# Last-layer messages of a graph network: the maximum with zero written in the form that also writes an accumulator

## What is computed

```python
src, dst = (edge_index[0], edge_index[1])
msg = jax.nn.relu(x[src] + edge_attr)
agg = jax.ops.segment_sum(msg, dst, num_segments=x.shape[0])
h = x + (x + agg)
f = _bn(h, bn1_gamma, bn1_beta, bn1_mean, bn1_var)
f = jax.nn.gelu(f @ W1.T + b1, approximate=False)
f = f @ W2.T + b2
return _bn(h + f, bn2_gamma, bn2_beta, bn2_mean, bn2_var)
```

## Time and profile before

| | |
|---|---|
| median of 3 runs | 7266.05 us (7260.23 to 7266.66) |
| profiled execution, its own time | 7249.92 us |
| its span, first to last instruction | 7247.8 us |
| busy share of the span: GpSimd (POOL) | 71% |
| TensorE (PE) | 63% |
| VectorE (DVE) | 37% |
| ScalarE (ACT) | 11% |

### The profile page before, as it was taken

The page is one execution under the profiler, slowest core; times in us unless marked ns, Lnnn a source line. Parts: engine busy times, 40 slices in busy tenths (PEclk is TensorE's granted clock), DMA queues, the critical chain, the costliest instruction groups (busy, mean ns, idle before and its releaser), DMA issues.

```text
span 7247.8 us, 61408 instructions
## 1 busy us (share of the span) xinstructions
PE 4554.3 (63%) x16502; PEld 3357.7 (46%) x16502; DVE 2695.0 (37%) x5977; ACT 831.1 (11%) x1870; POOL 5124.6 (71%) x4804
## 2 busy tenths in 40 slices
PE   4666559866666665555557656557655654565557
PEld 2455449654545454444435444445443443344336
DVE  6543111755555564421113211114111124444445
ACT  0000003323232222100000000000000000000002
POOL 5777760188888886477776777776777776777774
PEclk9888879988888887777878777778777777766779
DMA  2334334166666666433333333334333336666661
GB/s 77 102 116 118 105 111 136 20 72 72 71 71 72 72 72 115 151 105 105 105 105 120 104 105 105 105 105 124 105 105 105 105 105 190 194 195 194 195 192 51
DMA packets 495387, 810.82 MB, mean 112 GB/s; under 512 B 95107, under 2 KB 365333, under 8 KB 495061
## 3 DMA queue, kind: packets, MB, share of 16 engines
q0 software_dynamic: 300288, 615.29, 37.6%
q1 hardware_dynamic: 194772, 191.57, 8.2%
HBM read 652.63 MB, written 153.86 MB: 111 GB/s over the span
## 4 chain that ended last, share of the span: by engine, by line
POOL 60%; issue 22%; PE 9%; DVE 4%; DMA 3%; SPq 0%; ACT 0%; DVEq 0%; POOLq 0%; ACTq 0%
POOL ring L499 48%; POOL sums_by_src L521 12%; PE acc L560 2%; PE acc L641 2%; PE high L565 2%; DMA ring<-table_x,idx_dst 2%; PE acc L565 1%; DMA sums_by_src<-ring,E 1%; DVE H L1078 1%; PE high L560 1%; DVE ring L1199 1%; DVE onehot L1189 1%; DVE X L1220 0%; PE high L551 0%; PE acc L551 0%
## 5 line engine op out<-in xcount | busy, mean ns | idle before, releaser
L641 PE MATMUL acc<-ring,onehot 128*128 x8320 | 2897.0, 510 | 2040.1 <-DVE onehot L1189 2021.2
L641 PEld LDWEIGHTS acc<-ring,onehot 128*128 128x128 f32 x8320 | 2012.4, 253 | 2892.3 <-issue 2534.9
L499 POOL DMA_INDIRECT ring<-table_g,idx_dst x2346 | 2236.5, 953 | 887.8 <-issue 713.7
L1189 DVE TENSOR_TENSOR onehot<-iota_row,dl_dst 128x512 f32<-128x512 f32 x1040 | 719.3, 692 | 2959.3 <-SPq L284 2554.7
L521 POOL DMA_INDIRECT sums_by_src<-ring,E x782 | 1208.0, 1545 | 583.6 <-ACT high L989 344.2
L499 POOL DMA_INDIRECT ring<-table_x,idx_dst x782 | 823.5, 1053 | 269.3 <-issue 258.9
L499 POOL DMA_INDIRECT ring<-in_x_dram,idx_dst x782 | 781.0, 999 | 285.6 <-issue 253.2
L803 PE MATMUL high<-H,ring 128*128 x1664 | 545.3, 485 | 454.0 <-ACT high L989 439.0
L803 PEld LDWEIGHTS high<-H,ring 128*128 128x128 f32 x1664 | 374.9, 236 | 549.2 <-issue 489.5
L1431 DVE TENSOR_SCALAR ring<-acc,E 128x128 f32<-128x128 f32 x832 | 283.7, 402 | 573.5 <-PE acc L569 573.5
L1199 DVE TENSOR_TENSOR ring<-ring,E 128x1024 f32<-128x1024 f32 x196 | 239.9, 1224 | 541.1 <-DMA ring<-table_x,idx_dst 541.1
(11 more groups left out here) (269 smaller groups left out, 2856.7 us busy)
## 6 DMA issues: line engine op xcount, KB each, us to landing
E<-in_edge_attr_dram SPq DMA_DIRECT2D x781, 128.0 KB, 3.0
ring<-table_g,idx_dst POOLq DMA_INDIRECT x2346, 2.7
ring<-sums_by_src SPq DMA_DIRECT2D x36, 512.0 KB, 4.7
table_g<-H SPq DMA_DIRECT2D x36, 512.0 KB, 5.4
sums_by_src<-ring SPq DMA_DIRECT2D x2, 6272.0 KB, 39.2
ring<-in_x_dram,idx_dst POOLq DMA_INDIRECT x782, 2.8
sums_by_src<-ring,E POOLq DMA_INDIRECT x782, 3.8
ring<-table_x,idx_dst POOLq DMA_INDIRECT x782, 3.5
```

The lines of the kernel that those rows point to most:

```text
L499: pool.indirect_dma_start(out=ring_v[:, b % SLOTS, 0:D], out_offset=None, in_=table[name][:, :], in_offset=bass.IndirectOffsetOnAxis(ap=id ...
L641: pe.matmul(acc4[:, ds(to, width)], onehot[:, (q * BATCH + j) % ONEHOTS, :], ring[:, ds(slot, width)], start=False, stop=True, skip_group_ ...
L1189: last = tt(onehot[:, s:s + BATCH, :], iota_row[:, :].unsqueeze(1).to_broadcast((P, BATCH, P)), dl_ap[which][:, q * BATCH:(q + 1) * BATCH] ...
```

## The change

One line of `messages`. The maximum with zero gets a second operation, an addition of zero, as the reduction of an accumulator, and the accumulator goes to a column `dcol` that nothing reads any more at that point. What is written to the ring is the same. The order of instructions on every engine stays as it is.

```diff
                 link(tt(g, g, EA[:, at:at + here, :], ALU.add))
-                ts(g, g, 0.0, None, ALU.max).then_inc(sm("landed5"), here)
+                ts(g, g, 0.0, 0.0, ALU.max, ALU.add, accum_out=dcol[:, :]).then_inc(sm("landed5"), here)
```

## The result

| | before | changed |
|---|---|---|
| median of 5 runs each on one chip | 7266.05 us (7260.23 to 7268.06) | 7298.32 us (7294.30 to 7299.10) |
| profiled execution, its own time | 7249.92 us | 7298.68 us |
| its span | 7247.8 us | 7296.6 us |

The change makes the kernel slower by a ratio of 1.0045, 95% interval 1.0034 to 1.0056. That is 32 us; the forecast was 42 (7308 us).

A forecast was written before the change was run, and what follows sets the result against it. The last layer was taken as a gather chain on POOL with holds; a locked loop, (5.64 - 5.43) x 195 = +41 us plus 0.5 at the end, put 7266 + 42 at 7308 us, range 7195 to 7362.

The forecast's parts named there:

- What bounds the last layer: Last layer: a chain of gathers on POOL, 5.43 us a batch, 0.43 of it holds, mainly by ADD.
- counter-test: Last layer: a gather starting as ADD ends lies under all of MAX, takes 0.95 us; so ADD holds gathers.
- MAX's cost: VectorE, last layer: MAX grows from 0.695 to 1.21 us, 1.23 with read-out; +0.54 us a batch.
- VectorE's time is hidden: Last layer: VectorE's 3.26 us of a 5 us batch fit its idle time; only 0.5 us shows, once at the end.
- The form holds nothing: Accumulator MAX, last layer: holds no gather; taken alone 0.22 us less a batch.
- the first rival: Last layer: MAX holds the gathers, so all 83.7 us of holds vanish; 5.00 us a batch, 7182 us; chance 0.08.
- The loop: Last layer: each batch's third gather is held until ADD ends, locking every batch at 5.64 us; chance 0.64.
- the landing: Last layer: from the end of a batch's last gather to ADD's start, taken as 2.35 us, bounds 2.19 and 2.6.
- Slipping: Last layer: landings over 2.84 us let the third gather start before ADD unheld; 7231 or 7186 us; chance 0.14.
- The fourth rival: Last layer: accumulator MAX holds gathers too, some 0.5 us a batch; about +95 us, 7361 us; chance 0.05.

The follow-up runs named there:

- no_add: The changed kernel without the addition of the edge features, waiting for the step before; ratio 0.9902 to the kernel before, 5.07 us a batch.
- no_max: The kernel before without the maximum with zero, ADD itself releasing the feature loads; ratio 1.0050 to the kernel before, 5.60 us a batch.
- halves_loads_after_onehot: The kernel before with ADD and accumulator-form MAX each cut in two halves, feature loads waiting for the one-hot; ratio 0.9901, 5.09 us a batch.
- loads_after_matmul: The changed kernel with feature loads waiting for the first matmul behind the one-hot; ratio 0.9945 to the kernel before, 5.24 us a batch.
- plain_loads_after_matmul: The kernel before, MAX in plain form, with feature loads waiting for the step's first matmul; ratio 1.0005, 5.45 us a batch.
- plain_late: The kernel before, MAX in plain form, plus an idle accumulator instruction that delays the feature loads; ratio 1.0059, 5.66 us a batch.
- acc_loads_as_before: The changed kernel with MAX cut in two pieces, the first releasing the feature loads; ratio 0.9962 to the kernel before, 5.28 us a batch.
- loads_early: The changed kernel with feature loads released right behind ADD; ratio 1.0030 to the kernel before, 5.54 us a batch.
- loads_after_onehot: The changed kernel with feature loads waiting for the step's one-hot; ratio 1.0002 to the kernel before, 5.43 us a batch.

## Why the prediction was right

*What bounds the last layer.* Gathers and their holds: shown by no_add, which without ADD has 13 us of holds in place of the changed kernel's 114.6, and 5.07 us a batch in place of 5.59. The earlier trace rows had named the right holder, and no_max shows it directly. The earlier trace rows were a weaker counter-test than the prediction made of them: a gather that plain MAX holds back ends 0.12 us behind MAX's end, which there would be 6702.61, and this one ended at 6702.63 by itself. It shows only that MAX cost that gather nothing.

*MAX's cost.* 1.21 us and a read-out of 0.09 were forecast, 1.220 and 0.083 measured. That VectorE's time is hidden was right: the same instructions on VectorE gave 5.59 us a batch with one place of the loads and 5.24 with another, and halves_loads_after_onehot has the most VectorE work and the shortest batch of those that leave nothing out.

*The form holds nothing.* Right: the gather behind the held one takes a median of 0.949 us where it took 1.068 before, and held gathers end 0.82 us behind ADD's end instead of 0.92. The 0.22 us a batch that this was said to be worth, taken alone, came out as 0.21 between loads_after_matmul and plain_loads_after_matmul; it is not a fixed sum, since with the loads near their old place the form gave 0.15 (5.43 to 5.28), and with late loads 0.07 (plain_late's 5.66 to 5.59). Here the page "SBUF — State Buffer" of the Trainium skill (section "Who interferes with whom") was right on the form. Most of the hold, though, is the other clause's, the instruction with two SBUF inputs. Of the 0.43 us a batch that the first rival gave to MAX, MAX's own part was the 0.10 us by which held gathers now end sooner; 0.12 was the one-hot's, which the longer MAX moves behind the next gather's start. The late loads took more back than both. What the plain form does to a gather that starts under it is not shown: in the kernel before only one does, 0.02 us ahead of MAX's end.

*The loop.* Right: the held gather's end 0.82 behind ADD's, gap 0.30, gather 0.95, landing, ADD 1.23; each held gather the third of its batch; the loads 1.38 us behind ADD's end. The one batch of the trace before in which MAX had been late was a sample of the changed kernel: 5.74 us there, 5.59 in the mean now.

*The term that was off* is the landing: 2.35 us was assumed, the median is 2.28. With it the loop is 0.82 + 0.30 + 0.95 + 2.28 + 1.23 = 5.58 us instead of 5.64, which turns +41 us into +29; 31.0 was measured in the layer. The interval of the result, 25 to 41 us, just leaves the forecast of 42 out.

*The rivals.* Slipping does not happen in the changed kernel, since no landing ahead of a further batch reaches 2.84 us there (the longest is 2.72, nine in ten are under 2.44). It happens where landings of 2.8 to 3.1 us are common: in every other batch of the kernel before and of acc_loads_as_before, and in some of no_max and loads_early. The fourth rival, that the new form holds gathers, is out by the 0.949.

What was only argued: why a gather that ends about 1.5 us behind the first feature load lands latest. The runs show the dependence (median landing 1.90 us ahead of the loads, 2.13 at 0.1 behind, 2.28 at 0.7, 3.08 at 1.3, 2.77 at 2.0; from loads_after_matmul, loads_after_onehot, the changed kernel, acc_loads_as_before and loads_early). The DMA packets in these traces show where the time goes: each gather has 32 packets of 4 KB, and the last of them ends 1.52, 1.73, 1.82, 2.58 and 2.37 us behind the end of the gather's issue in these five cases, so that the landing follows 0.4 to 0.5 us later in each. Between the end of the issue and the gather's middle packet, 4, 0, 128, 307 and 354 packets of the feature loads start (medians). So late landings are late packets of the gather, and they come where many load packets run ahead of them; the last two cases stand in the other order, and which engine or memory makes the gather's packets wait stays open.

## What to carry to other kernels

Where GpSimd issues transfers back to back, look under which VectorE instruction each issue starts, and compare an issue that starts with that instruction against one that starts as it ends: two rows can tell which instruction holds it, if the rivals would end them at different times; a run that leaves the instruction out settles it. A change that removes a small hold can cost more than it gives if it moves the moment at which another queue starts its transfers, because the landing that closes the loop moves with it; time the release of a buffer by what its refill will collide with, not as early as possible. In a locked loop add up the terms from wait to wait, and look for one iteration of the old trace that already had the new timing.

## What the runs showed of the hardware that was not expected

An indirect DMA's issue on GpSimd stood still for the whole rest of a `tensor_tensor` with two SBUF inputs when it began under one (2.09 us instead of 0.95), but was not delayed when the same `tensor_tensor` began 0.1 us after it. The border is sharp, and lies a little behind ADD's start: in no_max gathers that began up to 0.042 us after ADD took 0.94 to 0.95 us, and the next, which began 0.045 us after it, took 2.00. The one-hot instruction, a `tensor_tensor` whose inputs are read by broadcast, held gathers in the same way: the 193 gathers that started under it in the kernel before ended 0.82 us behind its end (median), as far as held gathers end behind ADD's end in the changed kernel. And the latest place for the feature loads was better than the earliest: 5.24 us a batch at 3.13 us behind ADD's end against 5.54 at 0.08.
